# A gated cross-attention block on one core: attention in another order on every engine, products over all four quarters of the array, the first norm folded into the weights, and token rows laid partition by partition

## What is computed

```python
x = x + tanh(g_xattn[0]) * xattn(_layernorm(x), ctx, Wq, Wk, Wv, Wu, bu, qn_w, qn_b, kn_w, kn_b)
x = x + tanh(g_ffn[0]) * moe(_layernorm(x), Wg, W1, b1, W2, b2, Ws1, bs1, Ws2, bs2)

# xattn: 16 heads of 64
q = (emb @ Wq.T)  ; k = (context @ Wk.T) ; v = (context @ Wv.T)      # split in heads
q = _layernorm(q, qn_w, qn_b) ; k = _layernorm(k, kn_w, kn_b)        # over each head's 64
attn = softmax(einsum('bhqd,bhkd->bhqk', q, k) / 8)
out = einsum('bhqk,bhkd->bhqd', attn, v) ... @ Wu.T + bu

# moe: 8 experts of 512 hidden units, the 2 best per token, and a shared expert
```

## Time and profile before

| what | value |
|---|---|
| three runs | 815.65, 818.26, 818.64 us (median 818.26) |
| profiled execution | 812.57 us, its span 810.8 us |
| PE busy, weight loads busy | 681.3 us (84%), 599.5 us (74%) |
| DVE, ACT, POOL busy | 544.4 (67%), 435.0 (54%), 469.3 us (58%) |
| chain that ended last | PE 64%, DVE 11%, ACT 9%, issue 4%, another core or an unknown queue 4%, POOL 3%, DMA 2% |
| mean granted clock | 0.928 of full speed |

### The profile page before, as it was taken

The page is one execution under the profiler, slowest core; times in us unless marked ns, Lnnn a source line. Parts: engine busy times, 40 slices in busy tenths (PEclk is TensorE's granted clock), DMA queues, the critical chain, the costliest instruction groups (busy, mean ns, idle before and its releaser), DMA issues.

```text
span 810.8 us, 20629 instructions
## 1 busy us (share of the span) xinstructions
PE 681.3 (84%) x7762; PEld 599.5 (74%) x7762; DVE 544.4 (67%) x1315; ACT 435.0 (54%) x835; POOL 469.3 (58%) x487
## 2 busy tenths in 40 slices
PE   1778999999999999999999976877672699999960
PEld 1567888888888888888888765767562599999860
DVE  5656887888888888888888845666455244444426
ACT  2545767676666666676767642443240354445425
POOL 4564777777767676777777633345446155545540
PEclk9999999999999999999999995978886799999995
DMA  5152000000000000000000004001105222222229
GB/s 184 48 176 69 5 8 5 9 6 5 8 6 8 6 8 5 8 6 8 5 5 2 3 2 72 27 31 39 36 30 89 57 76 73 74 63 76 70 63 292
DMA packets 43854, 35.75 MB, mean 44 GB/s; under 512 B 5376, under 2 KB 37904, under 8 KB 43760
## 3 DMA queue, kind: packets, MB, share of 16 engines
q1 hardware_dynamic: 34912, 19.33, 9.0%
q0 software_dynamic: 4720, 9.89, 3.9%
q10 hardware_dynamic: 4128, 5.25, 2.4%
HBM read 21.04 MB, written 13.42 MB: 42 GB/s over the span
## 4 chain that ended last, share of the span: by engine, by line
PE 64%; DVE 11%; ACT 9%; issue 4%; another core or an unknown queue 4%; POOL 3%; DMA 2%; ACTq 1%; SPq 1%; DVEq 0%; POOLq 0%
PE ps L972 8%; PE ps L1076 8%; PE ps L922 8%; PE ps L893 7%; PE ps L876 5%; PE ps L878 5%; PE ps L877 5%; PE ps L985 4%; ACT spo L382 4%; PE ps L956 4%; ACT prob L389 4%; PE ps L1062 3%; PE ps L1064 3%; PE ps L1063 2%
## 5 line engine op out<-in xcount | busy, mean ns | idle before, releaser
L510 POOL TENSOR_TENSOR rstd<-var_eps,expo 128x16 f32<-128x16 f32 x64 | 186.3, 2911 | 5.0
L358 ACT ACTIVATE qk_T<-ps,lnw 128x512 f32<-128x512 f32 x128 | 96.5, 785 | 59.5 <-PE ps L893 59.3
L553 POOL DMA_INDIRECT results<-spo,xs_ix x78 | 75.2, 964 | 82.0 <-DVE spo L856 67.0
L536 POOL DMA_INDIRECT routed<-w_raw,slot x64 | 62.0, 969 | 69.4 <-issue 51.7
L441 ACT ACTIVATE qk_T<-ps,b_cols 128x256 f32<-128x256 f32 x156 | 61.5, 475 | 70.5 <-PE ps L1064 69.8
L876 PE MATMUL ps<-w_hi,xc_hi 128*128 128x512 f32 x192 | 91.9, 479 | 1.2 <-DVE prob L643 1.2
L664 DVE TENSOR_TENSOR wide<-ps,rstd 128x512 f32<-128x512 f32 x128 | 84.5, 683 | 8.9 <-POOL rstd L510 8.9
L893 PE MATMUL ps<-ident,wide 128*128 128x128 f32 x512 | 74.4, 279 | 12.5 <-DVE xc_lo L580 12.0
L508 POOL TENSOR_TENSOR var_eps<-ss,eps 128x16 f32<-128x16 f32 x64 | 14.0, 219 | 117.6 <-DVE ss L630 117.6
L630 DVE TENSOR_REDUCE ss<-wide 128x16 f32<-128x1024 f32 x64 | 77.4, 1210 | 4.5 <-ACT wide L366 3.3
L893 PEld LDWEIGHTS ps<-ident,wide 128*128 128x128 f32 x512 | 62.7, 145 | 23.0 <-issue 10.0
(11 more groups left out here) (169 smaller groups left out, 1524.6 us busy)
## 6 DMA issues: line engine op xcount, KB each, us to landing
v_sb<-routed SPq DMA_DIRECT2D x39, 129.0 KB
c_in<-in_ctx SPq DMA_DIRECT2D x32, 64.0 KB, 1.8
w_raw<-in_L_ffn_W ACTq DMA_DIRECT2D x1, 2048.0 KB, 8.5
wide<-results SPq DMA_DIRECT2D x8, 256.0 KB, 4.8
w_raw<-results SPq DMA_DIRECT2D x8, 256.0 KB, 4.8
out_x<-x_res SPq DMA_DIRECT2D x8, 256.0 KB, 4.1
results<-spo,xs_ix POOLq DMA_INDIRECT x78
routed<-w_raw,slot POOLq DMA_INDIRECT x64
```

Source lines behind the costliest of these rows:

```text
L358: nc.scalar.activation(qk_T[:, n, 4 * j:4 * j + 4, :].rearrange("p a n -> p (a n)"), ps[6 + j][:, :], ACT.Identity, bias=lnw[:, 2 * n + 1: ...
L510: nc.gpsimd.tensor_tensor(rstd[:, n, :], var_eps[:, n, :], expo[:, n, :], ALU.pow).then_inc(rstd_ready, 1)
L553: gp_.indirect_dma_start(out=results[:, :], out_offset=bass.IndirectOffsetOnAxis(ap=xs_ix[:, b4, a:a + 1], axis=0), in_=yb[:, b4, a, :], i ...
```

## The change

1. **Token layout.** The host hands `x` over as [128 partitions, 32 tiles, 128] and takes the output back so; it also hands over `x` and the context transposed (features by tokens), so that `xT` and `ctxT` are read in chunks of four tiles, 2 KB a partition. Row (partition p, tile t, choice c) of `results` is now (32p + t)*2 + c, and a group's two choices are read by one transfer with 4 KB a partition. `tok_i` numbers the rows accordingly.
2. **First norm folded.** PE no longer transposes tokens (L914, L915 are gone) and L618 and the power L499 are gone. Wq is centred over its input features by one product with I - 1/128. The division by the token's deviation drops out in the norm of each head of q, but for epsilon, which becomes 1e-5*(var + 1e-5) for each token (`token_eps`). The low part of the tokens is made by POOL from the loaded columns.
3. **Power replaced.** For q and k the -0.5 power L510 becomes ln and exp on ACT (`log_variance`, `inverse_root`) and a Newton step of four operations on POOL (`newton_step`).
4. **Four quarters.** The scores of pairs with even and odd number go to different banks and swap the column halves, so that consecutive products take turns over four quarters; `attend` alternates the sequences too. Scores of tile s and `attend` of tile s-1 now stand next to each other.
5. **Residual.** POOL adds the output bias into `x_res` beforehand, DVE adds the result in one operation.
6. **Order.** `step(s)` of every engine is a new list. The six loads of expert weights are all issued by ACT at the start of its step 1, the gates' loads and tanh come first on ACT. Several late tiles share the memory of `w_hi` and `w_lo`.

The lists and the functions that the prediction speaks of (cut):

```diff
 # PE
+            def scores(t):
...
+                    for a in range(PAIRS // 2):
+                        for b in range(2):
+                            for j in range(2):
+                                for h in range(2):
+                                    rows = slice(h * HD, (h + 1) * HD)
+                                    outs = slice((h ^ j) * HD, ((h ^ j) + 1) * HD)
+                                    last = nc.tensor.matmul(ps[4 + j][outs, (2 * a + b) * S:(2 * a + b + 1) * S],
+                                                            qk_T[rows, 0, 2 * a + j, b * S:(b + 1) * S],
+                                                            qk_T[rows, 1, 2 * a + j, b * S:(b + 1) * S], start=True, stop=True)
...
+            def before_k(j, t):
+                if j == 1 and has(t - 2):
+                    pe.wait_ge(y_read, t - 1)
+                else:
+                    pe.wait_ge(qT_ready[j], t + 1)
...
+            def step(s):
+                project_qk(0, 1, s + 1)
+                transpose_qk(0, 1, s, before_q)
+                project_v(1, s)
+                transpose_qk(0, 0, s, before_q)
+                project_v(0, s)
+                project_out(s - 2, before_y)
+                project_qk(1, 1, s + 1)
+                transpose_qk(1, 0, s, before_k)
+                transpose_qk(1, 1, s, before_k)
+                project_qk(1, 0, s + 1)
+                project_qk(0, 0, s + 2)
+                transpose_probabilities(0, s - 1, before_p)
+                transpose_probabilities(1, s - 1, before_p)
+                scores(s)
+                attend(s - 1)
 # ACT
+            def high_part(t):
+                if has(t):
+                    tokens, loaded = token_columns(t)
+                    sc.wait_ge(c_loaded[t // CK % 2], loaded)
+                    if t >= 2:
+                        sc.wait_ge(v_done[0], t - 1)
+                    nc.scalar.activation(xc_hi[:, t % 2, :, :], tokens, ACT.Copy).then_inc(xhi_ready, 1)
...
+            def step(s):
+                if s == 1:
+                    load_experts()
+                transposed(0, 0, s)
+                values(0, s)
+                square(1, 1, s + 1)
+                transposed(1, 0, s)
+                transposed(1, 1, s)
+                square(1, 0, s + 1)
+                probabilities(0, s - 1)
+                probabilities(1, s - 1)
+                expert_weights(s + 2)
+                square(0, 0, s + 2)
+                log_variance(1, s + 1)
+                inverse_root(1, s + 1)
+                outputs(1, s - 1)
+                outputs(0, s - 1)
+                square(0, 1, s + 2)
+                transposed(0, 1, s + 1)
+                high_part(s + 3)
+                exponential(s)
+                log_variance(0, s + 2)
+                values(1, s + 1)
+                inverse_root(0, s + 2)
 # POOL
+            def newton_step(n, t):
+                if has(t):
+                    gp_.wait_ge(root_ready[n], t + 1)
+                    nc.gpsimd.tensor_tensor(newton[:, n, :], root[:, n, :], root[:, n, :], ALU.mult).then_inc(nw_step[n], 1)
+                    gp_.wait_ge(nw_step[n], 4 * t + 2)
+                    nc.gpsimd.tensor_tensor(newton[:, n, :], newton[:, n, :], var_eps[:, n, :], ALU.mult).then_inc(nw_step[n], 1)
...
+                    nc.gpsimd.tensor_scalar(newton[:, n, :], newton[:, n, :], -0.5, 1.5, ALU.mult, ALU.add).then_inc(nw_step[n], 1)
...
+                    nc.gpsimd.tensor_tensor(rstd[:, n, :], root[:, n, :], newton[:, n, :], ALU.mult).then_inc(rstd_ready[n], 1)
...
+            def step(s):
+                variance(0, s)
+                newton_step(0, s)
+                normalise_rows(s - 2)
+                output_bias(s + 1)
+                variance(1, s)
+                newton_step(1, s)
+                expert_weights(s - 3)
+                second_rstd(s - 3)
+                token_eps(s + 1)
+                low_part(s + 2)
 # DVE
+            def step(s):
+                residual(s - 2)
+                token_statistics(s + 3)
+                scale(0, 0, s + 1)
+                scale(0, 1, s + 1)
+                sum_squares(1, s + 1)
+                second_statistics(s - 2)
+                maximum(1, s)
+                maximum(0, s)
+                less_maximum_of(1, s)
+                less_maximum_of(0, s)
+                sum_squares(0, s + 2)
+                scale(1, 1, s + 1)
+                scale(1, 0, s + 1)
+                row_sums(s)
+                row_inverses(s)
 # SP, the ending
-                for c in range(2):
-                    sp.dma_start(y_in[g][:, c, :, :], res_v[:, c, GT * g:GT * g + GT, :]).then_inc(o_in[g], 16)
+                sp.dma_start(y_in[g], res_v[:, GT * g:GT * g + GT, :, :]).then_inc(o_in[g], 16)
```

More of the change, by code:

```diff
@@ L24 @@
 GT = 4
+CK = 4
 GROUPS = TILES // GT
@@ L219, in flamingo_block, with steps @@
         STEADY = range(3, TILES - 3)
-        def steps(eng, step):
-            for s in range(-3, TILES + 2):
-                step(s, s % 2, s)
+        def steps(step):
+            for s in range(-5, TILES + 5):
+                step(s)
         W1_COLS = NX * FF
@@ new lines, in transposed @@
+            def transposed(n, j, t):
+                if has(t):
+                    if t == 0 and n == 0:
+                        sc.wait_ge(const_in, 10 * 16)
+                    sc.wait_ge(t_done[n][j], t + 1)
+                    if t >= 1:
+                        sc.wait_ge(s_done, t)
+                    nc.scalar.activation(qk_T[:, n, 4 * j:4 * j + 4, :].rearrange("p a n -> p (a n)"), ps[6 + j][:, :],
+                                         ACT.Identity, bias=lnw[:, 2 * n + 1:2 * n + 2], scale=lnw[:, 2 * n:2 * n + 1]).then_inc(T_ready[n][j], 1)
@@ L400, in hi_part @@
+            steps(step)
             def hi_part(g):
@@ new lines, in attend @@
+            def attend(t):
+                if has(t):
+                    for j in range(2):
+                        pe.wait_ge(pt_ready[j], t + 1)
+                    for p in range(PAIRS):
+                        at = p % 2 * (PAIRS // 2) + p // 2
+                        for h in range(2):
+                            for b in range(2):
+                                rows = slice(b * S, (b + 1) * S)
+                                q = (h ^ (p % 2)) * S
+                                last = nc.tensor.matmul(ps[6 + b][h * HD:(h + 1) * HD, p * S:(p + 1) * S],
+                                                        v_sb[rows, t % 2, (2 * p + h) * HD:(2 * p + h + 1) * HD],
+                                                        prob_T[rows, at, q:q + S], start=True, stop=True)
+                                if p == PAIRS - 1 and h == 1:
+                                    last.then_inc(o_done[b], 1)
@@ L919, in step, with project_out @@
+            def project_out(t, bank_free):
+                if has(t):
+                    bank_free(1, t)
+                    if t == 0:
                         pe.wait_ge(wu_in, 16)
-                    pe.wait_ge(o_ready, 2 * s - 2)
+                    for b in range(2):
+                        pe.wait_ge(o_ready[b], t + 1)
                     for p in range(PAIRS):
```

621 lines of the change are left out of this document (307 added, 314 removed).

## The result

The changed kernel takes **762.2 us** (median of four runs, 756.15 to 767.86) where the kernel before takes 818.45 on the same chip (815.65 to 820.44): a ratio of 0.928, 95% interval 0.922 to 0.935. The ratio leaves out the longest of the four runs, which was in the slower of the chip's two states. I forecast 794, and at least 772. The direction was right, the gain more than twice the forecast. The profiled execution took 764.29 us, with a span of 762.5.

The account below looks back on a forecast made before the run. PE at 98% was taken as attention's bound before, a 13.1 us loop of waits after. Attention -21, first steps -1 and ending -2 sum to -24: 818.3 - 24 = 794 us, range 772 to 815.

Parts of the forecast that it names:

- The 64x64 block: PE's scores and attention products in each attention step: 128 records at 28.8 ns, 3.68 us, near an issue bound of 25 ns.
- The far end: Low extreme for PE's 64x64 products: array-bound with twice the quarters, half of L985's price, 1.84 us.
- the rival to which I gave 0.10: Four quarters double the rate of PE's 64x64 products: 1.84 us, step 11.3, total 745 us; chance 0.10.
- PE's sum: PE's own work per attention step after the change: 8.81 plus 3.68 us for the 64x64 products, 12.5 us.
- The loop: Chain of waits through ACT, POOL and PE in an attention step, said to set the step at 13.1 us.
- The way back: PE's part of the attention step from transposing the probabilities to the next step's same v projection: 7.55 us.
- The two loops: Attention's wait chains through v's high part and through bank 6 for k's transposes, said to tie: 5.56 and 5.5 us.
- the slower rival: POOL's four Newton operations cost 0.55 us each, making the attention step 14.4 and the kernel 829 us; chance 0.07.
- nothing else is near: Attention before the change: PE busy 367.2 of 374.8 us, 98%, beside DVE 314, POOL 271 and ACT 255.
- The first steps: Start of the kernel: first powers drop out, Wv and the expert loads cost time; -1 us, ends -6 and +6.
- The ending: Final reads, DVE groups and last store: 2 us less, ends -5 and 0, with DVE's pace the next bound.
- the 350 GB/s that I had named as a sign: Ending: reads above 350 GB/s, with DVE groups 1.8 us apart from the start, were to show the forecast right.

Follow-up runs that it names:

- exp_first: Changed kernel with ScalarE's exponentials of tile s moved ahead of the high part of tile s+3: 744.15 us, ratio 0.907.
- q2: Changed kernel with its 64x64 products looped over two quarters at a time, in the loop order of the kernel before: 798.54 us, ratio 0.983.
- sp_loads: Changed kernel with the six expert loads issued by SyncE behind the second chunk of token columns, instead of by ScalarE: 749.6 us, ratio 0.913.
- old_rows: Changed kernel with token rows, results and output laid out in memory as in the kernel before: 768.95 us, ratio 0.930.
- power: Changed kernel with GpSimd's power of before in place of ln, root and the four Newton operations: 802.46 us, ratio 0.978.
- both: Changed kernel with exponentials ahead of the high part and the expert loads issued by SyncE: 718.98 us, ratio 0.885.
- q1: Changed kernel with its 64x64 products sorted by quarter, sixteen records in a row in the same one: 888.41 us in one run, ratio 1.095.
- q2_other: Changed kernel with its 64x64 products over two quarters at a time, in the other pairs (shared rows or columns): 795.27 us in one run, ratio 0.980.
- q2_power: Changed kernel with products over two quarters at a time and GpSimd's power in place of ln, root and Newton: 837.74 us, ratio 1.030.
- before_q4_exp: Kernel before with attention products over four quarters and ScalarE's exponentials ahead of both output copies: 805.41 us, ratio 0.993.

## Why the prediction was wrong where it was, and right where it was

**The 64x64 block: the step that failed.** "So I read about 25 ns as a bound of issue, L985 as nearly on it, and let four quarters gain only what brings scores to L985's price: 128 records x 28.8 ns = 3.68." It measured 2.02. The earlier trace rows show products that need all four quarters of the array; their 25 ns are no bound for products that leave three quarters free, which start 6 or 7 ns apart. The far end that I had named, half of L985's price or 1.84, was nearly it, and the rival to which I gave 0.10 was the case: it said 745 us, 17 below the median. Against the profiled executions it forecast -73 where -48 was measured: its step of 11.3 was 0.47 short, 13 us in 27 steps, its start 7, and the stalls 5. The means that I had, 34 and 29 ns with two quarters, did not decide it, but the trace of the kernel before does, record by record. L985 in time, cut off at 240.459 and at 240.465:

```profile
240.45 0.27 PE L985 MATMUL ps<-spo,v_sb 64*64 64x64 f32 x1
...
240.45 0.27 PE L985 MATMUL ps<-spo,v_sb 64*64 64x64 f32 x2
```

The second record has started within 12 ns of the first, and by 240.555 there is no third. From 200 to 350 us about half of the starts in L972 and L985 stand under 10 ns apart, and most of the others 51 or 52. So the floor of 25 ns agreed with the earlier trace rows alone, the close starts that I took to be shown by no run were in this trace, and a quarter's own pace of 58 ns, shared by four, could have been worked out from it.

**PE's sum.** 8.81 + 3.68 = 12.5 becomes 8.81 + 2.02 = 10.8; `exp_first`, in which TensorE hardly waits, has 11.06. **The loop.** From v's projection to the probabilities I laid out 5.56 us in ten terms; it measured 5.61 (227.66 to 233.27), with ln at 0.19 instead of 0.2 in the queue, the Newton step 1.07 instead of 1.1, and the product 1.91. The way back, 7.55, measured 6.16: 1.66 less by the block and 0.27 more, most of it the eight transposes of the probabilities (1.00 instead of 0.79). So 13.1 - 1.66 + 0.3 comes to 11.77 within the rounding. A step gained 2.10 us where I had 0.78. The two loops do tie, as written: each still shows its wait. `q2`, the world of the forecast with a block of 3.52, has 13.23 and a ratio of 0.983, or 805 us beside a kernel of 818.

**The Newton step** cost 0.20 to 0.22 an operation; the slower rival needed 0.47 (by its own terms 0.44: 14.0 less 13.1, over four, on top of 0.22). Its worth, 1.23 us a step, I had not priced at all, because a loop was laid out for the new kernel only and not for the kernel with one part left out. **A base that I misread:** "nothing else is near". Before, TensorE was 98% busy and the step was still held by loops at 13.87 and 13.71, since taking 0.75 of L985's 1.84 us away gained nothing; the loop at 13.71 goes through GpSimd, which was only 72% busy.

**The first steps.** I took -1, with +6 as the far end, and it was +6.2. The blocked issue was foreseen in its size (5.5 and "another 6", measured 11.18), but I booked most of it as covered. Nothing covered it: ScalarE had finished its step, and TensorE stood 16.05 us. The kernel before had lost some 7.5 us at such an issue itself (its second and third scores stand 21.35 us apart, not 13.87), which is why the net is no more than 6.2. `sp_loads` gets the tile back 15.1 us earlier. **The stalls.** Four steps between 76 and 164 us are 1.2 to 1.3 us longer, 5 in all, with TensorE stopped inside the block, at full granted clock and with no engine to wait for. No step of mine had them.

**The ending**: forecast -2, measured -2.1, and `old_rows` gives it back. VectorE's own pace of 1.78 is now the bound, as written, and the reads passed the 350 GB/s that I had named as a sign. **Expert rows** are 6.7 us longer in this one profile; over the fourteen profiled kernels this stage takes 146.5 to 160.1 us, and over the nine with the new rows alone 146.5 to 158.9, so it is not put down to the change.

The sum, with measured terms: 6.2 - 58.0 - 1.6 + 0.6 + 6.7 - 2.1 = -48.2, against -24.

## What to carry to other kernels

Before costing an array product that leaves rows and columns free, ask how many quarters consecutive products use, and look at the starts of single records; a floor read from products that fill the array is no floor for them. Price each part of a change in the loop with and without the other parts: in the new order two parts were worth 1.2 and 1.5 us a step, the quarters were worth nothing in a step of the old one (Newton was not tried there), and the change without these two parts lost 3%. And look for an engine's wait that stands in front of work that is ready (the exponentials behind the high part, the loads ahead of a queue that others wait for): these two moves took another 4.7% off.

## What the runs showed that I had not expected

- **Float32 products of 64x64 over one, two and four quarters**: 49.6, 27.5 and 15.8 ns a record, the same for the diagonal pairs as for pairs that share rows or columns. The Trainium skill, TensorE: Matmul & The Clock Gate, section "Measured speedup vs the span model", has packed tiles start some 4 ns apart; the traces show 6 or 7 ns between float32 products of 64x64 in different quarters. Its section "Wait — 56ns, not 53.3ns?" states a floor of about 25 ns between starts; for these products the runs contradict it.
- **Stalls inside the block.** Stalls that the profile lists, of 0.27 to 1.38 us, come only where the block is short: four in the changed kernel, two in `power`, `sp_loads`, `old_rows` and `both`, four in `exp_first`, none in `q2`, `q1`, `q2_other` and `q2_power` (a few blocks of `q2` and `q2_other` are 0.2 longer). The place moves back by two records every two tiles (after 50, 48, 46 and 44 records of L1049), which points to the instruction stream. In all four such steps of the changed kernel a packet of the instruction queue starts 0.3 to 0.6 us after the scores, and in the first step behind them without a stall 1.1 us before them. That is a coincidence in time; no run removes the cause.
- **A busy share of 98% says little about the bound.** The kernel before has it at 13.87 us a step, and `before_q4_exp` at 13.71 with 0.75 us less of work.
